# Layer 2's state loop: decays written to PSUM, B and C through one bank, one bank for the expert's first product

## The reference

```
dA  = exp(dt[..., None] * A)                     # decay, one per channel and state
dBu = (dt * u)[..., None] * Bm[:, :, None, :]
h   = dA_t * h + dBu_t                           # over the 512 positions
y   = einsum('lbin,bln->bli', h_seq, Cm)         # summed over the 16 states
...
x = x + s * silu(experts(xn))
```

## Time and profile before

| | before |
|---|---|
| median of 3 runs | 5828.37 us |
| lowest and highest run | 5816.56 and 5832.93 us |
| span of the profiled execution | 5822.4 us |
| PE busy | 4385.6 us (75%) |
| DVE busy | 4514.1 us (78%) |
| ACT busy | 2924.5 us (50%) |
| POOL busy | 2325.4 us (40%) |
| mean granted clock of PE | 0.895 |

### The profile page before, as it was taken

One profiled execution on the slowest core, in us unless ns is written; L12 is line 12 of the kernel. 1 busy time (PEld: TensorE's weight loads), 2 busy tenths in 40 slices (PEclk: granted clock), 3 DMA queues, 4 the chain that ended last, 5 costly groups with the idle time before them and its releaser, 6 DMA issues. The chain is left out here.

```text
span 5822.4 us, 60164 instructions
## 1 busy us (share of the span) xinstructions
PE 4385.6 (75%) x16724; PEld 2482.1 (43%) x16724; DVE 4514.1 (78%) x8572; ACT 2924.5 (50%) x5085; POOL 2325.4 (40%) x1980
## 2 busy tenths in 40 slices
PE   5876778767787677876778767787678866788776
PEld 1533435344353443534435344353444524444344
DVE  3678966789657996579965799658995489955898
ACT  3544645446444564445644456444564445645455
POOL 0134631447204562045620456104661046610565
PEclk9998889978899888998889988998889998899888
DMA  2000000000000000000000000000000000000000
GB/s 99 1 1 2 1 3 1 1 2 1 3 1 0 2 1 3 1 1 2 1 3 1 2 1 1 3 1 2 1 1 3 1 2 1 1 3 1 2 1 2
DMA packets 3537, 22.97 MB, mean 4 GB/s; under 512 B 336, under 2 KB 336, under 8 KB 2640
## 3 DMA queue, kind: packets, MB, share of 16 engines
q1 hardware_dynamic: 3152, 18.59, 0.8%
HBM read 16.23 MB, written 2.36 MB: 3 GB/s over the span
## 5 line engine op out<-in xcount | busy, mean ns | idle before, releaser
L1622 POOL TENSOR_SCALAR l_pp<-l_sc,l_m 128x512 f32<-128x512 f32 x496 | 783.4, 1579 | 644.3 <-DVE l_m L1572 596.7
L1572 DVE MAX8 l_m<-l_wk 128x8 f32<-128x512 f32 x1536 | 980.6, 680 | 0.0
L224 PE MATMUL bank<-l_v,l_pt 128*128 128x99 f32 (+1 forms) x5888 | 871.4, 300 | 139.5 <-ACT l_pt L1362 114.7
L224 PEld LDWEIGHTS bank<-l_v,l_pt 128*128 128x128 f32 x5888 | 814.9, 216 | 196.7 <-ACT l_pt L1362 154.0
L1316 PE MATMUL bank<-consts,l_pp 128*128 128x128 f32 x2048 | 390.9, 323 | 526.3 <-POOL l_pp L1629 519.8
L1180 POOL TENSOR_TENSOR l_hc<-l_h,l_cn 128x1024 f32<-128x1024 f32 x128 | 302.3, 2362 | 989.0 <-DVE l_h L1130 989.0
L1316 PEld LDWEIGHTS bank<-consts,l_pp 128*128 128x128 f32 x2048 | 280.2, 165 | 959.7 <-POOL l_pp L1629 828.2
L224 PE MATMUL bank<-l_km,hold 128*128 128x512 f32 x1024 | 652.7, 727 | 43.3 <-DVE l_ol L1539 18.1
L1568 DVE MATCH_REPLACE8 l_wk<-l_m,l_wk 128x512 f32<-128x512 f32 x1024 | 684.1, 675 | 0.0
L1392 ACT ACTIVATE l_sc<-bank 128x512 f32<-128x512 f32 x512 | 303.3, 594 | 739.9 <-PE bank L224 738.5
L1629 POOL TENSOR_TENSOR l_pp<-l_pp,l_ex 128x512 f32<-128x512 f32 x496 | 631.0, 1272 | 26.4 <-ACT l_ex L1399 5.7
(11 more groups left out here) (350 smaller groups left out, 8065.6 us busy)
## 6 DMA issues: line engine op xcount, KB each, us to landing
weights<-weights_dram SPq DMA_DIRECT2D x1, 11014.0 KB, 29.0
hold<-x_dram SPq DMA_DIRECT2D x9, 256.0 KB, 2.6
out_dram<-x SPq DMA_DIRECT2D x9, 256.0 KB, 3.4
consts<-consts_dram SPq DMA_DIRECT2D x1, 1503.0 KB, 32.2
rotary<-consts_dram SPq DMA_DIRECT2D x1, 1024.0 KB, 34.1
```

The source lines that it names most:

```text
L224: return nc.tensor.matmul(o, lhsT, rhs, start=start, stop=stop)
L1572: nc.vector.max(m8[n % RM][:, k + 1], wk_[n % 2][:]).then_inc(S["top"], 1)
L1622: nc.gpsimd.tensor_scalar(pp[n % 2][:], sc[n % RS][:], m8[n % RM][:, 3, 0:1], None, ALU.is_ge).then_inc(S["kept"], 1)
```

## The change

The decays `da` are no longer in SBUF. Half 0 is written to `bank[3]` and half 1 to `bank[7]`, with one buffer for each half. So the decay of half k of state n waits until the scan of half k of state n-1 has read the one before. To make these two banks free, C(n) goes to bank 2, after B(n) has been read by `db(n)`; B(n) waits until `cn` has read C(n-1); and the expert's first product always uses bank 4, so `w1(n)` waits for the DVE operation on the one before. C(n)'s matmul moves behind `w1(n)` and `gather(n-2)` in PE's order. The numbers of instructions on each engine stay as they are.

```diff
-                da, db, hh, hc = ([sb(f"l2_{n}{i}", [128, 2, T], c) for i in range(2)] for n in ("da", "db", "h", "hc"))
+                db, hh, hc = ([sb(f"l2_{n}{i}", [128, 2, T], c) for i in range(2)] for n in ("db", "h", "hc"))
+                da = [bank[3][:], bank[7][:]]
...
-                            if n >= 2:
-                                pe.wait_ge(S["silu"], n - 1)
-                            mm(bank[4 + 3 * (n % 2)][:], W(f"l2_w1_{e}", lo=128 * k, n=128), xn[:]).then_inc(S["w1"], 1)
+                            if n:
+                                pe.wait_ge(S["silu"], n)
+                            mm(bank[4][:], W(f"l2_w1_{e}", lo=128 * k, n=128), xn[:]).then_inc(S["w1"], 1)
...
                             if n:
-                                pe.wait_ge(S["db"], n)
+                                pe.wait_ge(S["cn"], n)
                             mm(bank[2][:], pick[:, n:n + 1].to_broadcast([96, 128]), parts[:]).then_inc(S["Bn"], 1)
-                            if n:
-                                pe.wait_ge(S["cn"], n)
-                            mm(bank[3][:], pick[:, NS + n:NS + n + 1].to_broadcast([96, 128]), parts[:]).then_inc(S["Cn"], 1)
                             if n:
                                 w1(n)
                             if n >= 2:
                                 gather(n - 2)
+                            pe.wait_ge(S["db"], n + 1)
+                            mm(bank[2][:], pick[:, NS + n:NS + n + 1].to_broadcast([96, 128]), parts[:]).then_inc(S["Cn"], 1)
...
-                            act(cn[n % 3][:], bank[3][:], ACT.Copy).then_inc(S["cn"], 1)
-                            if n >= 2:
-                                a.wait_ge(S["h"], 2 * n - 2)
+                            act(cn[n % 3][:], bank[2][:], ACT.Copy).then_inc(S["cn"], 1)
                             for k in range(2):
-                                act(da[n % 2][:, k], dt[:, k], ACT.Exp,
-                                    scale=a_neg[:, NS * k + n:NS * k + n + 1]).then_inc(S["da"], 1)
+                                if n:
+                                    a.wait_ge(S["h"], 2 * n + k - 1)
+                                act(da[k], dt[:, k], ACT.Exp, scale=a_neg[:, NS * k + n:NS * k + n + 1]).then_inc(S["da"], 1)
...
-                                nc.vector.tensor_tensor_scan(hh[n % 2][:, k], da[n % 2][:, k], db[n % 2][:, k], 0.0,
+                                nc.vector.tensor_tensor_scan(hh[n % 2][:, k], da[k], db[n % 2][:, k], 0.0,
```

More of the change, by code:

```diff
@@ L1023, in expert @@
                                 a.wait_ge(S["hg"], n - 1)
-                            act(h1[n % 2][:], bank[4 + 3 * (n % 2)][:], ACT.Tanh, scale=0.5).then_inc(S["h1"], 1)
+                            act(h1[n % 2][:], bank[4][:], ACT.Tanh, scale=0.5).then_inc(S["h1"], 1)
                         a.wait_ge(S["dt"], 2)
@@ L1135, in expert @@
                             v.wait_ge(S["h1"], n + 1)
-                            stt(h1[n % 2][:], h1[n % 2][:], 1.0, bank[4 + 3 * (n % 2)][:], ALU.add, ALU.mult).then_inc(S["silu"], 1)
+                            stt(h1[n % 2][:], h1[n % 2][:], 1.0, bank[4][:], ALU.add, ALU.mult).then_inc(S["silu"], 1)
                             v.wait_ge(S["silu"], n + 1)
```

## The result

The changed kernel takes 5907.15 us (median of 4 runs, 5899.67 to 5915.45) against 5822.47 us before: a ratio of 1.0148, 95% interval 1.0131 to 1.0165. It is slower by 85 us. The forecast was 5887 us, in a range of 5867 to 5923: 20 us too low. The forecast difference was 58 us, over a median before of 5828.37; that median is now 5822.47, with one more run, and the measured difference is 85. The profiled execution took 5899.67 us, the lowest of the four, with a span of 5897.5 us: 75.1 us more than the 5822.4 of before.

What follows compares the result with a forecast made beforehand. The prediction took DVE's instructions to bound the eight state loops, plus any waits between them. Its terms, -113.4 + 159.6 + 18.1 - 6.1 = +58.2 us, gave 5887 us, in a range of 5867 to 5923.

Steps and rivals of the forecast that it cites:

- Term 1, the collision: In the loops' scans on DVE: with decays in PSUM they no longer collide with POOL's y1, -113.4 us.
- The second reason that I gave: In the loops: y1 runs to about 3.75 us after a scan pair, next scans start at 3.69, leaving 0.06 us overlap.
- Term 2, the gap: Between scans and stt: DVE waits for the tanh, queued behind the waiting Exp; 1.33 us, 120 times, +159.6 us.
- Term 3, the start: First iteration of each loop: cn(0) waits for C(0) and db(0), so stt starts 2.26 us later, 8 times, +18.1 us.
- Term 4, ACT's writes: Exps on ACT that write PSUM: 0.045 us less each, 136 times, -6.1 us.
- Term 5, the scan's read from PSUM: Scans on DVE reading the decay from PSUM: taken as 0, bounded by 8 us either way.
- What the rest costs: nothing: Other new waits in the loop, on banks 2 and 4 and in PE's order: never late, so 0 us.
- rival (c): PE's clock falls in the loop: if half the iterations lost 1.40 us, 90 us more, 5977 us; chance 0.07.
- the high end: Upper end of the range: +95 us, 5923 us, allowing two lost clocks of 1.40 us per sequence, 22 us.
- my 167 us: Sign expected in the profile: DVE idle before the stt, about 1.2 us 120 times and 2.7 us 8 times.
- Rival (a): DVE's gap before the stt: the relief stays and the wait is hidden; -103, about 5725 us with no gap; chance 0.04.

## Why the prediction was right, and where it was off

**Term 1, the collision:** -113.4 forecast, -113.5 measured. The second reason that I gave was in fact nearly the whole: with the decays in SBUF only 6 us came back. I had 7 us, but for another cause: nothing came back in the ordinary iterations, where I had put 0.06 us each, and the 6 us are the last pairs, which aren't behind a db. So the size of that bound was right by luck.

**Term 2, the gap:** 1.33 us, measured 6.06 - 4.69 = 1.37. The hand-overs and the Exp and tanh are as worked out; only the stt that has waited takes 0.69 us in place of 0.66, so hg follows 0.03 later. 120 x 1.37 = 164 in place of 160. Taking the tanh out of the line removed the gap, and the Exp's wait alone made it: shown from both sides.

**Term 3, the start:** 2.26 us forecast, 2.70 measured (6.95 - 4.25 from du to the first scan). Two parts were too short. I had C(0) at full clock, 0.38 us; it took 0.61, after PE had waited 2.86 us for db, and with its hand-over that is 0.30 of the 0.44 missing. And cn(0) to the first Exp took 0.62 us, not 0.49. 8 x 2.70 = 22 in place of 18.

**Term 4, ACT's writes:** -6.1 forecast, 0 measured. The Exp is 0.03 us shorter, but the next instruction doesn't start sooner. The rows from which I took 0.045 us compared durations, of two instructions that differ in more than where the input lies (function and partitions, too), and what counts on this chain is start to start. What the Trainium skill states (ScalarE: Activation LUTs, "Step-by-step: what each stage is for"), that ACT writes faster to PSUM, shows as the shorter duration and is worth nothing here.

**Term 5, the scan's read from PSUM:** 0, as forecast; 1.207 us is the median after, 1.206 was the undisturbed mean.

**"What the rest costs: nothing"** is the step that was wrong in its reason. I put C's slack at 0.5 us because the second Exp is at 6.05 anyway. That cover was the new wait itself; without it, the shared bank 2 makes a gap of its own and costs 27 us in the loops, beside the 21 at their start. And the slack was too small for a low clock: rival (c) happened in part. PE stood idle for 1.88 us ahead of w1, not 1.7. The long iterations cost 17 us in the loops (two to five per sequence, up to 0.95 us each), about the 22 us that I had put at the high end. They are also most of what the stt waited beyond my 167 us: 195.0 in the changed kernel, 177.1 with more matmuls.

The sum as measured: -113.5 + 164 + 22 + 17 = +89.5, less 10.5 in stretches that weren't edited (from 75.1 - 64.2 - 21.4, with the loops at 703.7 and 767.9 from first scan to last, and the start); +79 against +75.1 in the spans. So the forecast time was close partly by luck: 31 us of cost missed in the terms, less 10 that came from stretches which no term is about. The 4 us between are near the few waits that the loops of before had of their own: DVE was idle before db and hg for 2.6 and 6.2 us, now 0.3 and 4.4. The medians of the runs differ by 85 us, 10 more than the spans, since the profiled run was the lowest of four. Why the unedited stretches take one length or another is not settled: they go with the granted clock, and no run here set it there.

Rival (a), the relief without the wait, isn't what this change did, but it is what the same change does with the tanh in another place: -88 us, ratio 0.9852. I had it at 5725 us with a gap of nothing, and the run gave 5738.

## What to carry to other kernels

When a buffer is made single, look at what stands in order behind the instruction that now waits; a tanh that had nothing to do with the decays cost 1.37 us an iteration, and one line moved turned +1.5% into -1.5%. When two waits end on the same instruction, undoing one shows nothing of its price; test each of them alone from the other kernel. A cover that the change itself makes is no cover for the next version: name it as such.

## What the runs showed that I had not expected

- A low granted clock of PE, 0.91 to 0.93 over the loop, cost nothing in the kernel where C isn't behind db (eight loops of 95.0 us each), and up to 0.95 us in an iteration in the one where it is.
- A higher clock in one stage came with a lower one in another. With five more matmuls per iteration the loops took 17 us less and the program 1 us less. The seven stretches between the loops, in which nothing was edited, came to 4379 to 4402 us over the kernels here. So under about 20 us the time of the whole doesn't judge an edit of this kernel; the loop's own length does.
- With both of a scan's inputs in SBUF, the scan and y1 don't share their time: the second waits for the first. In the last pairs with decays in SBUF y1 is first and keeps its 1.27 us; a scan that starts 0.09 us after it is 1.04 us longer, and one that starts 0.76 us after it 0.38: the two add up to 1.13 or 1.14 us in all eight.
